# Order of the shared expert's two layers in a cross-attention and mixture-of-experts kernel

## What is computed

```python
x = x + align(ctx, layernorm(x))
xf = layernorm(x).reshape(2048, 128)
scores = sigmoid(xf @ gate_w + bias)                 # 8 experts, best 2 of them
w = top-2 scores, normalised, at their experts
hact = gelu(einsum('th,ehi->tei', xf, up_w) + up_b)  # 512 hidden features
eo = einsum('tei,eih->teh', hact, down_w) + down_b
combined = einsum('teh,te->th', eo * 0.1, w)
shared = (gelu(xf @ sw_up + sb_up) @ sw_down + sb_down) * 0.1
out = shared + combined
x = x + out / (max(abs(out), axis=-1) + 1e-6)
```

## Time and profile before

| | us |
|---|---|
| median of 3 runs | 342.63 |
| lowest and highest | 338.51, 345.82 |
| the profiled execution, time | 343.59 |
| the profiled execution, span | 341.9 |
| PE busy | 175.6 |
| DVE busy | 197.6 |
| ACT busy | 124.3 |
| POOL busy | 114.1 |

### The profile page before, as it was taken

The page is one execution under the profiler, slowest core; times in us unless marked ns, Lnnn a source line. Parts: engine busy times, 40 slices in busy tenths (PEclk is TensorE's granted clock), DMA queues, the critical chain, the costliest instruction groups (busy, mean ns, idle before and its releaser), DMA issues.

```text
span 341.9 us, 5899 instructions
## 1 busy us (share of the span) xinstructions
PE 175.6 (51%) x1416; PEld 119.7 (35%) x1417; DVE 197.6 (58%) x931; ACT 124.3 (36%) x320; POOL 114.1 (33%) x210
## 2 busy tenths in 40 slices
PE   0850599700000047517842289898888788782000
PEld 0310244200000036403410056687677677572000
DVE  2937999997009358482710057585575676571192
ACT  5340399200003124815300032166556575561010
POOL 8000300000000130207777500047474747565251
PEclk9995599965555555557955569899999999997555
DMA  6029997950100000001111110122122122100732
GB/s 170 0 75 87 251 307 158 204 87 24 43 26 0 1 2 2 1 0 48 54 50 55 47 31 2 33 54 72 49 70 70 50 71 70 56 2 0 202 106 62
DMA packets 40069, 23.00 MB, mean 67 GB/s; under 512 B 14740, under 2 KB 37115, under 8 KB 40047
## 3 DMA queue, kind: packets, MB, share of 16 engines
q1 hardware_dynamic: 37176, 18.28, 23.3%
q0 software_dynamic: 2496, 4.24, 3.8%
q10 hardware_dynamic: 375, 0.24, 0.2%
HBM read 12.64 MB, written 11.03 MB: 69 GB/s over the span
## 4 chain that ended last, share of the span: by engine, by line
DVE 27%; PE 21%; issue 11%; DMA 11%; another core or an unknown queue 10%; ACT 10%; SPq 3%; ACTq 2%; DVEq 1%; POOL 1%; POOLq 0%
DMA choice_dram<-arena_f 5%; PE bank L940 5%; DVE arena_b L1090 5%; PE bank L938 4%; PE bank L939 4%; ACT arena_f L784 4%; DVE edge L1081 3%; SPq L419 2%; DVE arena_f L1085 2%; DVE arena_c L1082 2%; ACT row_and_place L747 2%; PE bank L960 2%; DVE arena_g L1319 2%; DVE x_sb L1366 2%
## 5 line engine op out<-in xcount | busy, mean ns | idle before, releaser
L644 POOL DMA_INDIRECT expert_dram<-arena_d,result_place x46 | 48.3, 1051 | 34.7 <-ACT arena_d L793 27.2
L940 PE MATMUL bank<-down_hi,arena_g 128*128 (+1 forms) x248 | 47.7, 223 | 2.7 <-issue 2.7
L784 ACT ACTIVATE arena_f<-bank,tile_bias 128x256 f32<-128x256 f32 x92 | 37.0, 496 | 15.2 <-remote 8.2
L938 PE MATMUL bank<-down_hi,arena_d 128*128 x184 | 35.9, 222 | 9.5 <-DVE arena_g L1319 7.3
L1317 DVE CAST arena_d<-arena_f 128x512 f16<-128x512 f32 x46 | 20.1, 438 | 29.2 <-ACT arena_f L784 21.5
L939 PE MATMUL bank<-arena_a,up_hi 128*128 128x256 f16 (+1 forms) x108 | 32.7, 303 | 3.7 <-issue 3.6
L939 PE MATMUL bank<-down_lo,arena_d 128*128 x184 | 34.6, 218 | 0.0
L1319 DVE TENSOR_TENSOR arena_g<-arena_f,arena_d 128x512 f16<-128x512 f32 x46 | 32.1, 699 | 1.6
L885 PE MATMUL bank<-arena_b,minus_one 128*128 (+1 forms) x26 | 3.9, 184 | 55.8 <-issue 55.7
L603 POOL COPY met_at<-arena_b 32x3 f16 (+1 forms) x26 | 3.9, 181 | 79.5 <-DVE arena_b L1150 75.3
L1290 DVE CAST arena_b<-arena_g 128x512 f16<-128x512 f32 x16 | 7.0, 437 | 38.3 <-ACT arena_g L769 38.3
(11 more groups left out here) (220 smaller groups left out, 475.9 us busy)
## 6 DMA issues: line engine op xcount, KB each, us to landing
sorted_dram<-padding SPq DMA_DIRECT2D x1, 3120.0 KB, 19.9
arena_g<-sorted_dram SPq DMA_DIRECT2D x24, 130.0 KB
arena_d<-in_L_ffn_up_w SPq DMA_DIRECT2D x6, 256.0 KB, 5.2
arena_d<-in_L_ffn_down_w SPq DMA_DIRECT2D x5, 256.0 KB, 5.3
x_sb<-in_x SPq DMA_DIRECT2D x4, 256.0 KB, 4.8
arena_b<-expert_dram SPq DMA_DIRECT2D x4, 256.0 KB, 4.5
arena_c<-expert_dram SPq DMA_DIRECT2D x4, 256.0 KB, 4.9
out<-x_sb SPq DMA_DIRECT2D x4, 256.0 KB, 2.3
```

The costliest lines, as they stand in the source:

```text
L644: pool.indirect_dma_start(out=expert_dram.ap(), in_=y_row[:, j % SLOTS, n, :], in_offset=None, out_offset=bass.IndirectOffsetOnAxis(ap=pla ...
L784: last = act.activation(hid[:, k, m, cols], banks[UP_BANK + HALVES * k + m][:, cols], ACT.Gelu, bias=bias, scale=1.0 / WSCALE)
L938: pe.matmul(o, a_hi, b_hi, start=start, stop=False)
L940: return pe.matmul(o, a_lo, b_hi, start=False, stop=stop)
```

## The change

All 16 up steps stand ahead of all 16 down steps on PE. For that the halves of all four batches must live at once, so a fourth home is added: its high halves at the end of `arena_f`, its low halves at the end of `arena_d`. DVE no longer copies batch 0 out between batch 2 and batch 3; all four copies stand behind its last split and behind the 10 small instructions that make the routed tiles' biases.

```diff
-S_SLOTS = 3
-S_LAG = NCH + 2
...
-        shared_hi, _ = within(arena_b, 0, (S_SLOTS, NCH, S), F16)
+        shared_hi = [within(arena_b, b * NCH * S // 2, (NCH, S), F16)[0] for b in range(B - 1)]
+        shared_hi.append(within(arena_f, 2 * B * S, (NCH, S), F16)[0])
...
-        shared_lo, at = within(arena_g, at, (S_SLOTS, NCH, S), F16)
+        shared_lo = []
+        for b in range(B - 1):
+            half, at = within(arena_g, at, (NCH, S), F16)
+            shared_lo.append(half)
+        shared_lo.append(within(arena_d, S_LAST, (NCH, S), F16)[0])
...
             def shared():
-                for m in range(B * NCH + S_LAG):
-                    if m < B * NCH:
-                        shared_up(m // NCH, m % NCH)
-                    if m >= S_LAG:
-                        shared_down((m - S_LAG) // TPB, (m - S_LAG) % TPB)
+                for m in range(B * NCH):
+                    shared_up(m // NCH, m % NCH)
+                for t in range(TILES):
+                    shared_down(t // TPB, t % TPB)
...
                 for n in range(B * NCH):
                     b, c = n // NCH, n % NCH
-                    if c == 0 and b >= S_SLOTS:
-                        keep_sum(b - S_SLOTS)
                     dve.wait_ge(s_gelu_done, n + 1)
...
-                keep_sum(B - S_SLOTS)
                 routed(dve.tensor_tensor(started[:], every_tile(tiles_before[:]), tile_nos, ALU.is_le))
...
-                for b in range(B - S_SLOTS + 1, B):
+                for b in range(B):
                     keep_sum(b)
```

More of the change, by code:

```diff
@@ L88, in build @@
         arena_a = sb("arena_a", [P, STEPS * (W + 1)])
-        arena_b = sb("arena_b", [P, max((STEPS + 1) * (W + 1), S_SLOTS * NCH * S // 2)])
+        arena_b = sb("arena_b", [P, max((STEPS + 1) * (W + 1), (B - 1) * NCH * S // 2)])
         arena_c = sb("arena_c", [P, STEPS * (W + 1)])
@@ L227, in build @@
         hid_hi, at = within(arena_d, TILES * H, (SLOTS, HALVES, I * PARTS // HALVES), F16)
-        shared_hi, _ = within(arena_b, 0, (S_SLOTS, NCH, S), F16)
+        shared_hi = [within(arena_b, b * NCH * S // 2, (NCH, S), F16)[0] for b in range(B - 1)]
+        shared_hi.append(within(arena_f, 2 * B * S, (NCH, S), F16)[0])
         y_row, at = within(arena_d, at, (SLOTS, PARTS, H))
         xT_hi, at = within(arena_d, at, (SLOTS, ET), F16)
+        S_LAST = at
         xT_lo, at = within(arena_a, TILES * P, (SLOTS, ET), F16)
@@ L963, in shared_down @@
                     h = slice(n * P, (n + 1) * P)
-                    mm = three_passes(o, shared_hi[:, b % S_SLOTS, c, h], shared_lo[:, b % S_SLOTS, c, h],
+                    mm = three_passes(o, shared_hi[b][:, c, h], shared_lo[b][:, c, h],
                                       down_hi[:, w], down_lo[:, w], False, c == NCH - 1)
@@ L1286, in shared @@
                     b, c = n // NCH, n % NCH
-                    if c == 0 and b >= S_SLOTS:
-                        keep_sum(b - S_SLOTS)
                     dve.wait_ge(s_gelu_done, n + 1)
-                    dve.tensor_copy(shared_hi[:, b % S_SLOTS, c, :], shared_g[:, n % 2, :]).then_inc(s_hi_ready, 1)
+                    dve.tensor_copy(shared_hi[b][:, c, :], shared_g[:, n % 2, :]).then_inc(s_hi_ready, 1)
                     dve.wait_ge(s_hi_ready, n + 1)
-                    dve.tensor_tensor(shared_lo[:, b % S_SLOTS, c, :], shared_g[:, n % 2, :],
-                                      shared_hi[:, b % S_SLOTS, c, :], ALU.subtract).then_inc(s_hid_ready, 1)
-                keep_sum(B - S_SLOTS)
+                    dve.tensor_tensor(shared_lo[b][:, c, :], shared_g[:, n % 2, :], shared_hi[b][:, c, :], ALU.subtract
+                                      ).then_inc(s_hid_ready, 1)
                 routed(dve.tensor_tensor(started[:], every_tile(tiles_before[:]), tile_nos, ALU.is_le))
```

## The result

The changed kernel took 352.23 us (median of 4 runs, 349.94 to 358.76), the kernel before 341.81 us: the ratio is 1.0295 with a 95% interval of 1.0212 to 1.0378, slower. The forecast was 339.2 us, within 323 to 347 us. The profiled execution of the changed kernel took 353.0 us, its span is 351.3 us, 9.4 us more than before.

A forecast was written before the change was run, and what follows sets the result against it. The shared expert on PE, not the scatter, was taken to hold back the routed stage. Profiled 343.6 us less 3.9 us from reordering, 0 us for fourth home and copies, gave 339.7 us, adjusted to 339.2 us; range 323 to 347 us.

The forecast's parts named there:

- slow stretch: Shared expert, up to 198.45 us: finished-matmul signals come late and PE starts only 29 matmuls in 28 us.
- After it: Down steps behind the release at 198.45 us: 4.75 us at half clock, then full clock; end 213.9 us, 3.9 us gained.
- Up steps first: Shared expert's start: up steps pass unslowed every 1.07 us, so down steps start at 175.4 us.
- second rival: Shared expert: up steps are caught, late signals cost 12 to 14 us each; 5.0 us slower, 348.6 us; chance 0.14.
- turning point: Shared expert: a loss as soon as fewer than about 1.5 down steps have passed by the release.
- dense short matmuls: Shared expert: short matmuls beside steady indirect DMAs bring on the slow stretch; long ones at the gelus' pace do not.
- first rival: Shared expert: no slow stretch in the new order, down steps end at 194.5 us; 323.5 us in all; chance 0.18.
- The two rules: Skill pages on PE: TensorE never waits on anyone, about 323 us; or reporting finished instructions stalls it, gain nearer 2.5 us.

The follow-up runs named there:

- old order: Changed kernel with PE's and DVE's order of before, four homes kept, PE waiting for the second routed-token load before the twelfth up step: 343.7 us.
- changed kernel with 128 rows: Changed kernel with the down steps' bias matmuls zero-padded from 9 to 128 rows: 339.95 and 334.61 us with signals late, 304.49 us on time.
- held kernels: PE also waits for the second routed-token load: changed kernel 351.86 and 355.17 us, with 128-row bias matmuls 339.84 us; order of before with four homes 343.7 us.

## Why the prediction was wrong

What was right: the shared expert on PE sets the start of the routed experts, the slow stretch comes again in the new order and ends near 198 us, and behind the transposes nothing changes (123.7 against 123.3 us). The fourth home cost nothing that shows (first transposes at 218.28 against 218.60 us in the old order). The moved copies cost nothing in the measured kernel, where the transposes follow the last down step by the same 0.83 us as before. That they are covered is a matter of when down steps run: in the profile of the changed kernel with 128 rows and signals on time, batch 2's first down step waits for the first copy.

```profile
184.30 0.46 PE L966 MATMUL bank<-down_b_all,arena_f 128*128 128x128 f32 x2 [0.91 <-DVE arena_d L1287]
```

The step that failed is "After it": "The clock is at half for 4.75 us, in which a down step takes 1.98 us: 2.4 steps. The other 9.0 take 1.19 us." The 4.75 us were taken from a stretch with up steps in it and applied to one without. In their place the clock stayed at half for all of it: behind 198.2 us stood 13.6 down steps, and 13.6 x 2.11 = 28.7 us, which is where it ended (226.7 us). At the old recovery the same steps would have ended near 216 us (198.2 + 4.75 + 11.3 x 1.19 = 216.4 us), 1.4 us ahead of before. So some 10 us of the 12.8 us between forecast (213.9 us) and measurement (226.7 us) are the clock. The held kernels bear that out: 10.2 us between the first transposes of new and old order, and 15.9 against 27.4 us from release to transposes with 128 and 9 rows.

The rest, 2.5 us, is the step "Up steps first". Up steps did fall into the slow stretch, so the last ended at 183.5 us instead of 175.4 us, and 2.4 down steps passed by the release, not 4.6. That is the second rival's mechanism in a milder form: gelus 11 to 15 follow each other after 2.1 to 5.6 us, not 12 to 14 us. That rival's size was wrong, and by its own turning point (1.5 steps) it alone would still have given no loss. The trigger that I read from the rows, "dense short matmuls", was wrong as a rule: up steps alone can be caught too, here from about 170 us. But the onset varies: the same kernel with the wait started 15 matmuls from 170.5 to 184 us in one profile and 63 in another, both on chips with late signals. In four of the nine profiles of the new order on such chips the last gelu starts by 178.7 us, near its 177.6 us with signals on time, so there the up steps went through as the prediction had it. What sets the onset stays open.

The first rival named a kernel without a slow stretch at 323 us. It exists, on three of the six chips of the experiments, at 304 to 305 us. Its reason was missed even so: it is not the new order that brings it about, since the old one is as fast there. That the routed loop was slowed too (158 matmuls in 16.1 us against 202) was in the earlier trace rows, and I read it as the loop's own pace.

The two rules. The Trainium skill, page "SBUF — State Buffer", section "Who interferes with whom", has TensorE never wait on anyone; it speaks of access to that memory. On three chips that agrees with PE beside the same scatters (no late signal); on the others it does not describe what the trace shows, 29 matmuls in 28 us. The Trainium skill's page "NOTIFIC — the notification-queue block", section "7.1 Overflow: three behaviours, one of which stalls the engine", tells of a setting in which a full queue of records stalls the engine. No run here looked into that path. Why some chips are slow is open.

## What to carry to other kernels

When work is reordered, ask what the new neighbours do to TensorE's clock: a busy engine is not enough, and a stretch that got its clock back before did so with the matmuls that stood in it then. Here a 9-row matmul at the head of every step kept a stage that began at half clock there for 25 us and more, and left one that began at full clock alone; padding it to all rows with zeros cost a memset. And before a profile's strange stretch is taken as the kernel's own, look whether the kernel before takes the same time on another chip.

## What the runs showed of the hardware

- TensorE at 0.50 granted clock for over 28 us of unbroken work (198.2 to 226.8 us, 28.5 us busy of 28.6 us), and again in both held kernels with 9 rows, for 27.5 us in one and for 25.4 us in the other, where it then rose among the same steps.
- The same steps at 1.00 for 19.1 us where they began at full clock (changed kernel, signals on time).
- The same down step with its float32 bias matmul on 128 instead of 9 rows: 0.95 against 1.19 us at full clock.
- The kernel before takes 304 to 305 us (medians) on three chips, and 341 to 346 us on three others and in the result; its runs on one chip spread by about 2%. In the first profile of the latter kind gelus of the shared expert start late beside indirect DMAs, by up to some 24 us behind the modelled end of their matmuls. The cause was not found.
